# Two graph convolutions: GpSimd waits behind each group of eight gathers until all eight have landed, and tells TensorE of it at once

## What is computed

```python
def gcn_conv(x, W, b, src, dst, n_nodes):
    h = x @ W
    deg = segment_sum(ones, dst, n_nodes) + 1.0
    dinv = rsqrt(deg)
    norm = dinv[src] * dinv[dst]
    msg = h[src] * norm[:, None]
    agg = segment_sum(msg, dst, n_nodes)
    return agg + h * (dinv * dinv)[:, None] + b

h1 = relu(gcn_conv(embedding, W1, b1, src, dst, n))   # 256 -> 64
h2 = relu(gcn_conv(h1, W2, b2, src, dst, n))          # 64 -> 256
```

## Time and profile before

| | us |
|---|---|
| timed runs, median of 3 | 5349.65 |
| lowest and highest | 5347.81, 5350.41 |
| span of the profiled execution | 5935.3 |
| of it: first convolution | 1211.0 |
| of it: second convolution | 1191.0 |
| GpSimd busy in the span | 3055.9 |
| TensorE busy with matmuls | 3546.3 |

### The profile page before, as it was taken

One profiled execution on the slowest core, in us unless ns is written; L12 is line 12 of the kernel. 1 busy time (PEld: TensorE's weight loads), 2 busy tenths in 40 slices (PEclk: granted clock), 3 DMA queues, 4 the chain that ended last, 5 costly groups with the idle time before them and its releaser, 6 DMA issues. The chain is left out here.

```text
span 5935.3 us, 66919 instructions
## 1 busy us (share of the span) xinstructions
PE 3546.3 (60%) x13782; PEld 2710.2 (46%) x13783; DVE 2982.8 (50%) x6982; ACT 1018.9 (17%) x2146; POOL 3055.9 (51%) x2888
## 2 busy tenths in 40 slices
PE   4744455454389865998444544454445454466998
PEld 3633233232267654776433433333434444455666
DVE  5466566666899964445433333334333333354443
ACT  0111121121179801221000000000000000013121
POOL 1266677676368624221466666663666666612111
PEclk9877767776599976998566566655555555566999
DMA  4487666666578762223311111111111111123221
GB/s 108 136 217 211 202 207 203 204 206 195 158 227 271 224 188 88 63 63 97 106 28 28 29 28 28 29 29 32 28 29 28 28 29 28 29 62 98 70 87 37
DMA packets 432122, 617.01 MB, mean 104 GB/s; under 512 B 100329, under 2 KB 309161, under 8 KB 431721
## 3 DMA queue, kind: packets, MB, share of 16 engines
q1 hardware_dynamic: 304733, 389.03, 21.1%
q0 software_dynamic: 107440, 200.97, 14.1%
q10 hardware_dynamic: 19852, 25.94, 1.6%
HBM read 419.67 MB, written 209.64 MB: 106 GB/s over the span
## 5 line engine op out<-in xcount | busy, mean ns | idle before, releaser
L1857 POOL DMA_INDIRECT big<-t_d,src_tiles x1564 | 1483.7, 949 | 957.2 <-issue 450.8
L2080 PE MATMUL v_bank<-big,v_oh 128*128 x3328 | 716.2, 390 | 1216.6 <-issue 830.3
L2080 PEld LDWEIGHTS v_bank<-big,v_oh 128*128 128x128 f32 x3328 | 674.7, 300 | 1302.8 <-issue 1302.2
L653 POOL DMA_INDIRECT big<-xl_d,src_steps x832 | 859.8, 1033 | 378.1 <-issue 356.0
L1935 DVE TENSOR_TENSOR big<-big,v_bank 128x64 f32 x1664 | 366.5, 220 | 1285.3 <-DMA xj_d<-big 973.2
L759 PE MATMUL se_z_ps<-big,se_oht 128*128 x1664 | 608.7, 517 | 628.5 <-issue 385.9
L759 PEld LDWEIGHTS se_z_ps<-big,se_oht 128*128 128x128 f32 x1664 | 386.8, 250 | 850.4 <-issue 780.7
L692 DVE TENSOR_TENSOR se_z<-se_z_ps,big 128x528 f32<-128x528 f32 x416 | 291.4, 700 | 461.1 <-DMA es_ts<-src_p 256.8
L1122 PE MATMUL ae_bank<-ae_v,ae_oh 128*128 128x266 f32 x1664 | 402.3, 397 | 49.8 <-DVE big L1106 36.7
L1081 POOL TENSOR_TENSOR ae_v<-ae_v,ex 128x1792 f32<-128x1792 f32 x104 | 334.1, 3215 | 178.1 <-DMA ae_v<-xj_d 178.0
L1122 PEld LDWEIGHTS ae_bank<-ae_v,ae_oh 128*128 128x128 f32 x1664 | 310.4, 191 | 141.5 <-DVE big L1106 53.0
(11 more groups left out here) (468 smaller groups left out, 5316.9 us busy)
## 6 DMA issues: line engine op xcount, KB each, us to landing
xj_d<-big SPq DMA_DIRECT2D x208, 528.0 KB
ae_v<-xj_d SPq DMA_DIRECT2D x208, 528.0 KB
se_dlb<-dlr_d SPq DMA_DIRECT2D x104, 256.0 KB
big<-t_d,src_tiles POOLq DMA_INDIRECT x1564
buf_d<-ne_blank SPq DMA_DIRECT2D x4, 4112.0 KB
e_xs<-buf_d SPq DMA_DIRECT2D x106, 129.0 KB, 2.1
big<-xl_d,src_steps POOLq DMA_INDIRECT x832
cp_y<-y_d SPq DMA_DIRECT2D x14, 896.0 KB, 7.4
```

What stands on the lines that cost most here:

```text
L653: nc.gpsimd.indirect_dma_start(half_of(u)[:, k, :], None, table, bass.IndirectOffsetOnAxis(ap=m.src[:, t:t + 1], axis=0)).then_inc(landed[ ...
L1857: nc.gpsimd.indirect_dma_start(rows[:, t % RING, :], None, table, bass.IndirectOffsetOnAxis(ap=m.srct[:, t:t + 1], axis=0)).then_inc(lande ...
L2080: last = nc.tensor.matmul(bank[u][:, k * MH:(k + 1) * MH], oh[:, u, k, :], of_block(rows, at[k]), start=True, stop=True)
```

## The change

The wait ahead of group g is now for group g-1 and no longer for g-2, from g = 1 on, and the increment of `tiles_in` stands right behind it. So it comes after the eight gathers of g-1 have been issued and ahead of the eight of g. The value that is waited for is that of all gathers of the same parity up to group g-1. After the loop one group is left to wait for and to tell of, where there were two. Nothing else differs: the wait for `summed`, the gathers, their order, the ring and the other engines' programs are as they were.

```diff
                 for g in range(TG):
-                    if g >= 2:
-                        pool.wait_ge(landed[g % 2], 16 * GS * (g // 2))
+                    if g >= 1:
+                        pool.wait_ge(landed[(g - 1) % 2], 16 * GS * ((g + 1) // 2))
                         pool.sem_inc(s["tiles_in"], 1)
                     if g + NB // GS + 2 > RING // GS:
                         pool.wait_ge(s["summed"], g + NB // GS + 2 - RING // GS)
                     for t in range(g * GS, min((g + 1) * GS, NT)):
                         nc.gpsimd.indirect_dma_start(rows[:, t % RING, :], None, table,
                                                      bass.IndirectOffsetOnAxis(ap=m.srct[:, t:t + 1], axis=0)).then_inc(landed[g % 2], 16)
-                for g in (TG - 2, TG - 1):
-                    pool.wait_ge(landed[g % 2], 16 * (GS * (g // 2) + min(GS, NT - g * GS)))
-                    pool.sem_inc(s["tiles_in"], 1)
+                pool.wait_ge(landed[(TG - 1) % 2], 16 * (GS * ((TG - 1) // 2) + NT - (TG - 1) * GS))
+                pool.sem_inc(s["tiles_in"], 1)
```

## The result

The changed kernel takes 5734.77 us (median of 4 runs, 5731.98 to 5736.39), beside 5350.03 us for the kernel before: a ratio of 1.0711 [1.0696, 1.0725], some 385 us slower. The forecast was 277 us slower, 5627; its range ended at 5665. Direction and place were right, the price of one stop was too small: 385 / 194 is 1.98 us a group, where 1.43 had been worked out.

A forecast was written before the change was run, and what follows sets the result against it. The prediction took GpSimd's gathers to bound the convolutions at 19.98 us a pair of groups. With 194 groups each longer by 1.43 us, 277 us, it forecast 5349.65 + 277 = 5627 us, range 5420 to 5665.

The forecast's parts named there:

- the price of one stop: GpSimd, ahead of each group: landing 1.5 plus restart 0.23 less today's gap 0.30, 1.43 us, 194 times, 277 us.
- GpSimd is the bound at 19.98 us a pair: Both convolutions: timed runs issue gathers back to back, two groups of eight in 19.98 us, while TensorE waits for tiles.
- The 585.65 us: Whole kernel: the first profiled execution, 5935.3 us, exceeds the timed median, 5349.65; at least 77 us must come from the convolutions.
- The landing, 1.5 us (1.36 to 1.66): Ahead of each group: time from the end of the last gather until its landing is seen by the wait.
- Restarting costs 0.23 us: GpSimd, ahead of each group: from the semaphore instruction at 5203.5 to the next gather's start at 5203.73.
- The bounds of the restart: Ahead of each group: restart taken as 0.23 us alone, within a growth of 1.29 to 1.59 us a group.
- Telling at once: GpSimd telling TensorE of tiles: looks like 10 us gained, claimed none; rival that TensorE hears sooner: 5332 us, chance 0.05.
- The last two waits become one: After each convolution's loop: costs nothing, since both waits are met when the last gather lands.
- The profiled span should move by little: Profiled run: GpSimd's pair becomes 22.84 us, still under TensorE's 23.3, so the span of 5935.3 us hardly moves.
- the sharpest sign: Changed kernel's trace: convolutions keep their 1211 and 1191 us while the timed runs grow, if TensorE still paces the profiled run.
- The signs in the trace: Changed kernel's gathers: about 1.7 us or more ahead of every group, none at 0.30, landing named, gathers within groups keep 0.94 + 0.30.

The follow-up runs named there:

- the kernel in which the gather waits itself: Changed kernel with the telling moved behind the next group's first gather and the wait on `summed` to the previous group's fifth gather: 5652.68 us, 1.0548.
- the wait behind two gathers: Changed kernel with the wait and the telling moved behind the second gather of the next group: 5358.78 us, 1.0008 of the kernel before.
- the profile taken again: The kernel before, unchanged, profiled once more: the run took 5352.88 us and spans 5351.2 us.
- the one with its stop in the same place: Changed kernel with the wait and the telling moved behind the first gather of the next group: 5515.39 us, 1.0308 of the kernel before.
- the kernel with the marks: Changed kernel with GpSimd also counting up a spare semaphore behind each group's first, fourth and eighth gather: 5748.48 us in one run.

## Why the prediction was right and wrong

- **GpSimd is the bound at 19.98 us a pair.** Right, against the rows of a profile that said otherwise. The 585.65 us that did not fit gave only bounds, 77 to 392 us from the convolutions; the upper end was a choice and not worked out. It came out: between the two profiles of the kernel before the convolutions differ by 382.4 us. The estimate of some 1005 us for a convolution stands beside 1015.9 and 1003.7 measured.
- **The landing, 1.5 us (1.36 to 1.66).** Right: 1.47.
- **"Restarting costs 0.23 us".** This is the step that failed. It measured 0.75, and 194 x 0.52 is 101 us of the 108 that were missing; what remains is small and told below. The row behind it is of a gather that carries its own wait, on `summed`; the telling that it was counted from the earlier trace rows is the line's last and belongs to the group after, so it stands in the stream behind that group's eight gathers and not ahead of them. A restart of that kind does cost so little (0.26 in the runs). The change puts its wait on another kind of instruction: the wait is on the telling, and the gather stands behind the telling. The price was looked up for the right engine and the wrong instruction, and the 0.5 us of making the gather ready behind the telling stood at nothing in the sum. What the prediction worked out, 277 us, is the price of the kernel in which the gather waits itself: its gaps came to 283.
 The Trainium skill (Perfetto Trace Analysis, Per-engine timelines) tells the two kinds apart: an instruction of the sequencer alone waits for its semaphores in the sequencer, which fetches the next one only afterwards, while a DMA of GpSimd is decoded, pushed into a wait queue and waits there. The traces agree, with 0.77 us against 0.26; the page gives no times, and what the half microsecond of making ready is spent on, no run shows.
- **The bounds of the restart.** It had none: the range of 1.29 to 1.59 us a stop came from the landing alone, and one pair of rows gave the restart for both ends.
- **"Telling at once" is no gain.** Right. In the kernel before the telling ran 1.53 us (median of 192) after the last gather it tells of, in the changed one 1.47, and the wait behind two gathers, with its early telling, gained nothing.
- **The last two waits become one, at nothing.** Right: from the last gather of one convolution to the first of the next 26.7 us before and 25.1 after.
- **The profiled span should move by little.** Wrong, and it had been called the sharpest sign. It took the first profiled execution for what profiling does to this kernel. In the profile taken again, and in those of the ten changed kernels, the profiled execution is 1.7 us longer than its span, and where a kernel has other runs, as long as they are. The Trainium skill (Runtime: NRT & Kernel Launch, The ~15µs preamble/postamble breakdown) has a gap of about 6.2 us, the same for every kernel, between a profile's total time and the reported execution time. That total time is not the span, and no run here shows it. The prediction let the 585 us speak against this rule; they say only that that one execution was another than the timed ones. That the changed kernel's convolutions, 1202.5 and 1194.8 us, come near the 1211.0 and 1191.0 of the earlier trace rows, as the sign wanted, is chance: GpSimd's landings fill them, and not TensorE's pace.
- **The signs in the trace.** No group follows at 0.30 us, a landing is named ahead of nearly every group, gathers keep 0.94 + 0.30: right. The gap is 2.2 us, over the "about 1.7 or more".

The remainder is small: 372 us of gaps, 5.5 us of somewhat longer gathers and 4 us in the last stage, less 3 us in the stages ahead, make the 379 us between the two spans; the timed runs say 385.

## What to carry to other kernels

When a wait is added, ask which instruction carries it: on GpSimd here, a gather behind a waiting semaphore instruction was made ready only after the wait, while a gather that carried the wait itself had that part behind it. A wait for one's own last transfer, directly behind it, costs landing plus restart at every turn; with two further gathers issued between the transfer and the wait, it cost nothing here. And where one profile is far from the timed runs, profile again before reading waits from it, or, if that can't be done, work out as here what the timed runs allow.

## What the hardware showed beside

- A gather occupies GpSimd's instruction stream for 0.47 to 0.53 us beside the 0.94 us of its work; the two run side by side as long as the stream is ahead, and add up only behind a stop.
- The second gather of six groups in each convolution (14, 28, 42, 56, 70, 84) comes some 2.1 us after the first, in all kernels but the one with its stop in the same place (there 3.7 to 4.0; in the first profile of the kernel before 0.6 to 2.1), and also where three marks a group stand in the stream. So it goes by the number of gathers and not by that of instructions. It is the stream that stands still: in the kernel with the marks, the mark behind the fourth gather of these groups comes 4.7 us after the telling, and not 1.96. The cause was not tried.
- A landing takes as long after four gathers as after eight, 1.48 us, so the gathers of a group do not pile up behind one another. Together with its own 0.94 us a 32 KB gather takes 2.4 us. The Trainium skill (DMA: Bandwidth & Descriptors, Anatomy of one DMA) gives an estimate of 2.08 us for it, 0.3 too little here.
